# Gate and up of the second tile as a Strassen product, its z sums and all weight sums made in the first tile

## The reference, cut to what matters

```
def qlinear(x, q, scale, A, B):              # low rank part beside a quantised one
    w = (q - 7.5) * (scale * 0.005)[:, None]
    return x @ w.T + 0.02 * (x @ A @ B)
def ffn(x): return qlinear(silu(qlinear(x, gate...)) * qlinear(x, up...), down...)   # 512 -> 1376 -> 512
x = x + 0.5 * ffn(layernorm(x))
x = x + s4(layernorm(x))      # a causal convolution of each row with one kernel row of 512, and D * u
x = x + 0.5 * ffn(layernorm(x))              # the same weights
```

## Time and profile before

| | |
|---|---|
| runs | 589.48 us median of 3 (586.4, 589.48, 589.52) |
| profiled execution, its own time | 588.72 us |
| its span | 586.7 us |
| busy in the span | PE 566.7 us (97%), PEld 436.4 (74%), VectorE 403.0 (69%), ScalarE 303.2 (52%), POOL 229.5 (39%) |
| mean granted TensorE clock | 0.993 |

### The profile page before, as it was taken

One profiled execution on the slowest core, in us unless ns is written; L12 is line 12 of the kernel. 1 busy time (PEld: TensorE's weight loads), 2 busy tenths in 40 slices (PEclk: granted clock), 3 DMA queues, 4 the chain that ended last, 5 costly groups with the idle time before them and its releaser, 6 DMA issues.

```text
span 586.7 us, 12166 instructions
## 1 busy us (share of the span) xinstructions
PE 566.7 (97%) x4656; PEld 436.4 (74%) x4656; DVE 403.0 (69%) x766; ACT 303.2 (52%) x748; POOL 229.5 (39%) x248
## 2 busy tenths in 40 slices
PE   6799998999989999999999999999999999999996
PEld 6544675436678887888778887788877888788975
DVE  6577864886489867599576995479844888455544
ACT  5476412666238851478505784158831676236621
POOL 5446500030205980059701596026850367105510
PEclk9899998999999999999999999999999999999999
DMA  8983302003323074001820019000190202540001
GB/s 287 374 272 120 72 11 69 13 0 64 73 15 14 12 112 86 10 1 20 146 44 10 2 20 177 13 11 1 26 178 11 77 1 43 94 149 5 1 2 73
DMA packets 87266, 39.75 MB, mean 68 GB/s; under 512 B 75849, under 2 KB 80713, under 8 KB 87209
## 3 DMA queue, kind: packets, MB, share of 16 engines
q1 hardware_dynamic: 86393, 38.84, 29.5%
q10 hardware_dynamic: 816, 0.14, 0.1%
HBM read 16.42 MB, written 4.19 MB: 35 GB/s over the span
## 4 chain that ended last, share of the span: by engine, by line
PE 91%; DVE 4%; ACT 2%; issue 1%; DVEq 1%; DMA 1%; ACTq 0%
PE banks L1436 35%; PE banks L1359 28%; PE banks L1419 11%; PE banks L1401 5%; PE banks L1565 4%; PE banks L1324 3%; PE banks L1378 2%; PE banks L1395 1%; ACT p_stack L638 1%; DVEq L858 1%; DMA X<-in_x 1%; PE banks L1554 1%; DVE stats L857 1%; PE banks L1585 0%; DVE zs L869 0%
## 5 line engine op out<-in xcount | busy, mean ns | idle before, releaser
L1436 PE MATMUL banks<-xT,w 128*128 128x256 f16 (+1 forms) x1848 | 223.1, 273 | 1.3 <-DVE ring L996 1.3
L1436 PEld LDWEIGHTS banks<-xT,w 128*128 128x128 f16 (+1 forms) x1848 | 182.0, 100 | 22.7 <-issue 1.8
L1359 PE MATMUL banks<-dw,hT 128*128 128x256 f16 (+3 forms) x1408 | 184.8, 286 | 0.0
L1359 PEld LDWEIGHTS banks<-dw,hT 128*128 128x128 f16 (+1 forms) x1408 | 135.7, 98 | 35.0 <-issue 0.9
L955 DVE SCALAR_TENSOR_TENSOR work<-banks,work 128x512 f32<-128x512 f32 (+1 forms) x88 | 60.6, 689 | 59.3 <-PE banks L1401 25.5
L483 POOL TENSOR_TENSOR rstd<-veps,minus_half 128x1 f32<-128x1 f32 x32 | 19.9, 623 | 182.3 <-DVE veps L861 182.1
L1419 PE MATMUL banks<-xT,w 128*128 128x512 f16 (+1 forms) x336 | 80.0, 382 | 1.6 <-DVE work L955 0.7
L554 POOL TENSOR_TENSOR hT<-work,hT 128x512 f16<-128x512 f32 x60 | 70.8, 1181 | 5.0
L551 POOL TENSOR_SCALAR hT<-work 128x512 f16<-128x512 f32 x60 | 37.8, 630 | 89.1 <-DVE work L955 89.1
L1419 PEld LDWEIGHTS banks<-xT,w 128*128 128x128 f16 (+1 forms) x336 | 33.4, 101 | 42.3 <-ACT work L687 2.6
L638 ACT ACTIVATE p_stack<-banks 128x64 f16<-128x64 f32 x96 | 14.6, 226 | 88.2 <-PE banks L1324 83.5
(11 more groups left out here) (176 smaller groups left out, 704.0 us busy)
## 6 DMA issues: line engine op xcount, KB each, us to landing
out_x<-X SPq DMA_DIRECT2D x16, 256.0 KB, 2.6
X<-in_x SPq DMA_DIRECT2D x1, 2048.0 KB, 8.5
ring<-in_gate_q_t SPq DMA_DIRECT2D x2, 768.0 KB, 12.4
hT<-in_up_q_t SPq DMA_DIRECT2D x2, 768.0 KB, 13.1
work<-in_b SPq DMA_DIRECT2D x2, 688.0 KB, 8.8
X<-in_x SPq DMA_DIRECT2D x4, 256.0 KB, 5.1
X<-in_x SPq DMA_DIRECT2D x1, 1024.0 KB, 13.3
ring<-in_down_q_t SPq DMA_DIRECT2D x1, 1024.0 KB, 11.7
```

What stands on the lines that cost most here:

```text
L1359: last = mm(acc(j)[:, 1 - c, 0:width], hT[0:rows[m], m, a, j * P:(j + 1) * P], dw[0:rows[m], m, src], start=(m == 0 and a == 0), stop=(m = ...
L1436: last = mm(dst[0:r, 0:HH], w[:, blocks + k, cols], xT[:, a, 2 * op + k, :], start=(first and k == 0 and a == 0), stop=(k == 1 and a == 1) ...
```

## The change

- FAST is 1: tile 1 uses fast blocks. S4_TILE = 1 keeps the S4 steps at tile 1. The x transposes of tile 1 by subtiles go, four quarter transposes take their place.
- The z sums of tile 1 and all weight sums are made in tile 0, among its plain blocks and at its end.
- The S4 steps of VectorE move out of the blocks: s4_vectors ahead of the first pd_split of tile 0, s4_sums(0) and (1) to the end of tile 0, the rest ahead of the first pd_split of tile 1. The small product of the S4 vector B (`state_b`) moves into the blocks of tile 0.
- In fast tiles a p product makes its B11, B21 or T1 + B22 part only; VectorE copies B11 from PSUM (once for two subtiles) and adds (`p_sum`), and p_high and p_split read the sum. On ScalarE pd_copy 1 and 3 now stand before p_high.
- B's raw values go to the last half of X instead of `work`, loaded in two parts of columns; ScalarE makes the high half of the first, POOL that of the second. SP's load of that half of X waits for s_bw.
- The start: 96 and 28 warm matmuls for 60 and 12, another order of the first products, x_out(1) on VectorE, two z copies on ScalarE, block 1's products before the last p transpose and the low rank of block 0.

```diff
-    FAST = 2
+    FAST = 1
+    S4_TILE = 1
 # SP
+            sp.wait_ge(s_bw, 4)
             sp.dma_start(X[:, 2 * TS:SUBS, :], x_v[:, 2 * TS:SUBS, :]).then_inc(s_xrest[1], 16)
...
-                if n + 1 < FAST:
-                    sp.wait_ge(f.u_mm, (n + 1) * M)
-                    x_transposes(n + 1)
 # POOL
+            cast_gate(1)
             for g, wb in enumerate((gb_w, ub_w)):
-                pool.wait_ge(s_lrb[g], 16)
-                pool.tensor_scalar(wb[:, :], b_raw[:, g, :], B_SCALE, 0.0, ...
+                pool.wait_ge(s_lrb[1][g], 16)
+                pool.tensor_scalar(wb[:, b_parts[1]], b_raw[:, g, b_parts[1]], B_SCALE, 0.0, ...
-            for c in range(1, len(CHUNKS)):
+            for c in range(2, len(CHUNKS)):
                 cast_gate(c)
+            ln_rstd(1, 0, 1, 2, 3)
             for m in range(M):
                 if m == DQ:
-                    ln_rstd(1, 0, 1)
+                    z_low(1, 0, 0)
+                    z_low(1, 0, 1)
...
-            ln_rstd(1, 2, 3)
             s4_norms()
...
             s4_resolvents()
-            ln_rstd(2, 0, 1)
...
+            z_low(1, 1, 0)
+            z_low(1, 1, 1)
 # ScalarE, plain_blocks
-                    if n == 0 and m in (0, 2, 4):
+                    if n == 0 and m == 0:
+                        p_out(2)
+                        p_out(3)
+                    if n == 0 and m in (2, 4):
                         cast_up(1 + m // 2)
-                    if n + 1 == FAST and 3 <= m <= 6:
-                        z_high(n + 1, 0, m - 3)
+                    if 4 <= m <= 7:
+                        z_high(n + 1, 0, m - 4)
 # VectorE
+            def p_sum(n, i):
+                dve.wait_ge(f.p_mm, n * TS + i + 1)
+                after(dve, f.p_hi, n * TS + i)
+                own = slice(4 * R * (1 + i % 2), 4 * R * (2 + i % 2))
+                if i % 2 == 0:
+                    V.tensor_copy(p_b11, p_bank(n, i)[:, 0:4 * R]).then_inc(f.p_b11, 1)
+                    dve.wait_ge(f.p_b11, ((n - FAST) * TS + i) // 2 + 1)
+                V.tensor_tensor(p32, p_bank(n, i)[:, own], p_b11, ALU.add).then_inc(f.p_sum, 1)
...
+                    if m == 2:
+                        dve.wait_ge(s_xrest[0], 16)
+                    if m in (2, 3, 4):
+                        ln_stats(1, *((0, 1), (2,), (3,))[m - 2])
+                    if m in (3, 9):
+                        z_apply(1, m // 9)
+                    if m in (4, 10):
+                        z_differences(1, m // 10)
+                    if m == 5:
+                        z_sums(1, 0)
+                    if m in (5, 7):
+                        weight_sum(0, m // 7)
...
+                    if m == 8:
+                        weight_sum(1, 0, 1)
...
 # VectorE, tile's end
                 if n == 0:
+                    z_sums(1, 1)
                     s4_inverse()
+                    s4_b_copy()
+                    s4_vectors()
+                if s4:
+                    s4_sums(2)
+                    s4_roots(0)
+                    s4_roots(1)
+                    s4_fold()
                 pd_split(n, 0)
                 down_read(n, 0)
                 pd_split(n, 1)
                 if more:
+                    p_sum(n + 1, 0)
                     p_split(n + 1, 0)
...
                 down_add(n, 2)
+                if n == 0:
+                    weight_sum(3, 0, 1)
...
                 if more:
+                    p_sum(n + 1, 2)
                     p_split(n + 1, 2)
                 pd_split(n, 3)
...
                 down_add(n, 3)
+                if n == 0:
+                    s4_sums(0)
+                    s4_sums(1)
 # TensorE
+                elif i % 2 == 0:
+                    sums(0, half(B11, 0))
+                    last = sums(1, half(B21, 2))
                 else:
+                    last = sums(2, half(T1, 0) + half(B22, 2))
...
+                if n == 0:
+                    product(n, 0, 1)
+                    p_transpose(3)
+                    product(n, 1, 1)
                     for g in range(2):
+                        low_rank(n, g, 0)
...
-            warm(60)
+            warm(96)
             x_transpose(0, 0, 2)
-            warm(12)
+            warm(28)
             x_transpose(1, 1, 3)
             pe.wait_ge(s_aw, 1)
             p_product(0, 0)
+            p_product(0, 1)
             first_products(0)
             x_transpose(2, 2, 2)
-            p_product(0, 1)
+            first_products(1)
             x_transpose(3, 3, 3)
-            first_products(1)
             p_product(0, 2)
             p_transpose(0)
-            p_transpose(1)
             first_products(2)
             p_product(0, 3)
+            p_transpose(1)
             first_products(3)
             p_transpose(2)
-            p_transpose(3)
```

More of the change, by code:

```diff
@@ L223, in s4_macaron @@
         s_lr = sem("low_rank_a_loaded")
-        s_lrb = [sem(f"low_rank_b_{g}_loaded") for g in ("gate", "up")]
+        s_lrb = [[sem(f"low_rank_b_{g}_part{c}_loaded") for g in ("gate", "up")] for c in range(2)]
         s_lrd = sem("low_rank_down_loaded")
@@ L586, in _ @@
             s4_resolvents()
-            ln_rstd(2, 0, 1)
-            z_low(2, 0, 0)
-            ln_rstd(2, 2)
-            z_low(2, 0, 1)
-            ln_rstd(2, 3)
-            z_low(2, 1, 0)
-            z_low(2, 1, 1)
+            z_low(1, 1, 0)
+            z_low(1, 1, 1)
             for n in range(FAST, N2):
@@ L830, in _ @@
             cast_up(0)
-            x_out(1, 1, 3)
+            z_first_high(2)
             p_high(0, 0)
+            z_first_high(3)
+            p_high(0, 1)
+            low_rank_b_high(0)
+            low_rank_b_high(1)
             x_out(2, 2, 2)
-            p_high(0, 1)
             p_high(0, 2)
             p_out(0)
+            cast_up(1)
+            p_high(0, 3)
             p_out(1)
-            p_high(0, 3)
-            p_out(2)
-            p_out(3)
             act.wait_ge(s_scales, 1)
-            act.wait_ge(s_bw, 2)
             for n in range(N2):
@@ L1050, in fast_blocks @@
                 for m in range(M + 1):
+                    if n == S4_TILE and m == 0:
+                        dve.wait_ge(s_xrest[1], 16)
                     if m:
@@ L1097, in tile @@
                     conv_add(c * TS + 3)
-                if n == 0:
-                    s4_vectors()
                 if s4:
@@ L1102, in tile @@
                 if more:
+                    p_sum(n + 1, 3)
                     p_split(n + 1, 3)
@@ L1498, in tile @@
                 down_pass(n, 1, 1, LATE)
-                if n == 0:
-                    pe.wait_ge(s_kin, 128)
-                    for v in range(2):
-                        last = mm(bank[0][:, v:v + 1], vct[:, v, :], bp, start=True, stop=True)
-                    last.then_inc(s_bmm, 1)
                 down_low(n, 0)
@@ L1535, in tile, with state_b @@
                 down_low(n, 3)
+            def state_b():
+                pe.wait_ge(s_kin, 128)
+                for v in range(2):
+                    last = mm(bank[4][:, v:v + 1], vct[:, v, :], bp, start=True, stop=True)
+                last.then_inc(s_bmm, 1)
             def cauchy():
@@ L1553, in kernel_row @@
                     for c in range(2):
-                        last = mm(bank[0][0:1, :], fold[:, 4 + c, k:k + 1], tab[:, c, k, :],
+                        last = mm(bank[3][0:1, :], fold[:, 4 + c, k:k + 1], tab[:, c, k, :],
                                   start=(k == 0 and c == 0), stop=(k == 1 and c == 1))
```

171 lines of the change are left out of this document (77 added, 94 removed).

## The result

The changed kernel takes 594.73 us (median of 4 runs, 592.72 to 594.93) beside 587.94 us for the kernel before on the same chip (586.18 to 589.52): ratio 1.0117, 95% interval 1.0094 to 1.0139. It is 1.2% slower; the prediction said 582, faster, and its range ended at 588.

What follows compares the result with a forecast made beforehand. TensorE, carrying 91% of the chain of waits, was taken to bound the kernel. Terms -4.4 + 1.5 + 4.6 - 6.2 - 1.1 - 1.3 = -6.9 took 588.7 to 581.8, forecast 582 us, range 575.5 to 588.

Steps and rivals of the forecast that it cites:

- the first tile's end: First tile's end: POOL's norms delay VectorE, p_product(1,3) waits 3.3 us; +4.6 us, bounds -1.2 and 7.
- POOL's norms: First tile's end: POOL's s4_norms take 13.3 us and end at 73.0, with VectorE waiting for them.
- The slow clock behind a gap is paid before and after alike: First tile's end: both kernels pay the slow clock behind a gap, so nothing was charged for it.
- Start: Start, up to block 2: more warm matmuls and a new order bring block 2 earlier; -4.4 us, bounds -1 and -5.
- Rival B: Start: warm matmuls and new hand-overs hold it as long as before; -1 for -4.4, 585.2 us, chance 0.24.
- First tile's blocks: First tile's blocks: added z work delays ScalarE by 1.0 and 0.6 us; +1.5 us, bounds 0 and 2.5.
- Second tile's blocks: Second tile's blocks: Strassen's 38.40 us replaces plain's 44.63; -6.2 us, bounds -5 and -6.3.
- Second tile's end: Second tile's end: loses the dsum wait, gains from p, pays 0.5 us for S4 work; -1.1 us.
- Rival D: Second tile's end: S4 group starts only after both z_low; +2.1 for +0.5, 583.4 us, chance 0.10.
- Later boundaries: Five later tile boundaries: shorter p products gain 0.26 us each; -1.3 us, bounds -3.7 and +1.
- A (VectorE not late): First tile's end: POOL's norms finish before z_sums or PSUM reads go faster; -1.2 for +4.6, 576 us, chance 0.21.
- C: Seven boundaries: p sums stand on the path and cost 1.5 us at each; slower, 592.5 us, chance 0.06.

Runs made afterwards that it cites:

- e6: Changed kernel with only POOL's queue reordered: down casts start before the last two rstds, second z_low two casts later; 591.86 us, ratio 1.0068.
- e1: Changed kernel with VectorE's copy of the S4 product B made first, before z_sums and the reciprocal; 593.26 us, ratio 1.0107.
- e2: e1 with s4_vectors back at its old place, ahead of the last p split; 589.20 us, ratio 1.0037.
- e10: Changed kernel with conv_stats(0,2) behind pd_split(0,3) and weight_sum(3) behind p_split(1,3); 591.51 us, ratio 1.0080.
- e13: Changed kernel with the old p products, without sums on VectorE, at all seven boundaries; 589.26 us, ratio 1.0049.
- A: As a kernel: the changed kernel itself, against the kernel before; 594.73 us, ratio 1.0117.
- e4: Kernel before with the new start alone; second tile, S4 and p products as before; 587.98 us, ratio 1.0014.
- e12: e11 with p sums again from the fourth tile on, weight_sum(3) ahead of the reciprocal, S4 vectors behind down_add(0,2); 578.91 us, ratio 0.9852.
- e11: e9 with the old p products, without sums on VectorE, at all seven boundaries; 579.67 us, ratio 0.9876.
- e9: e8 with conv_stats(0,2) behind pd_split(0,3) and weight_sum(3) behind p_split(1,3); 583.43 us, ratio 0.9936.
- e8: Changed kernel with earlier POOL casts and memsets, b copy in block 9, vectors ahead of the reciprocal, weight sums 2 and 3 moved; 585.57 us, ratio 0.9960.

## Why the prediction was wrong

The step that failed is **the first tile's end**, +4.6 where +14.2 was measured: the length of VectorE's queue ahead of pd_split(0,0) and of p_product(1,3), with a wait on it that was not seen and a slow clock that was put at nothing. "VectorE waits there ... then reciprocal 1.74, b copy, s4_vectors 2.4 ...: 78.0. Behind them stands pd_split(0,0) ... 1.4 late." The chain was right in kind (VectorE idle for POOL, then late, and p_product(1,3) waiting for p_stack), and so were several of the signs. Its sizes were not, and one wait was missing:

- POOL's norms. The forecast has them end 7.5 us behind the start of the tile's end (73.0 less the old 65.55); they end 10.3 behind it (73.52 less 63.23), 2.8 late. POOL's queue from the last rstd to the norms' end takes 29.5 us (44.04 to 73.52) where I had 25.8 (48.6 to 74.4): the norms 14.5 for 13.3, the last four casts 4.3 where I had written 3.0 (58.1 to 61.1) although my own 0.83 each makes 3.3, z_low 4.15 for 3.72. e6, which touches POOL's queue alone, gives 2.9 us back, 1.2 of it in the blocks (the tile's end starts at 62.00 for 63.23).
- The missed wait. I asked who waits for pd_split but not who waits for the b copy. The diff adds a wait on TensorE for it, ahead of the down pass of subtile 1. I had the old trace's free TensorE up to 76.78 in its place. e1 shows that this changed where TensorE stood rather than how long (593.26, and a span of 591.9 for 593.1), since VectorE is late at the next thing that it owes as well.
- VectorE's own work was under-sized. The vectors take 6.7 us and not 2.4 (moving them, e2, gives 4.1 us of the kernel's time). The sums of p and the weight sums ahead of the last split were counted; they made a wait of 4.05 for the 3.3 forecast, on top of all that came before it, and slow clock behind it (e10 gives 2.2 us back by the ratios, e13 4.0). I had the row that warned and used it at the second tile's end, where nothing was held.
- "The slow clock behind a gap is paid before and after alike": no. Before pays it once, over some 3 us (granted clock 0.63, 0.50, 0.50 and 0.67 in the four us from 93 to 97); A pays it twice: 2.75 us on 48 down matmuls (8.87 against 6.12 in e1), 1.8 on the rest of the tile's end and 2.4 on the second tile's first block (7.56 against 5.18).

The others, in order:

- **Start**, -4.4 for -5.6: right, somewhat better, since the 96 warm matmuls took 7.42 us and ended at 9.4, not 10.2. Rival B's main reason was wrong, but e4 shows the gain can be lost a few blocks on.
- **First tile's blocks**, +1.5 for +3.2. Of the two waits at ScalarE, forecast as 1.0 and 0.6, the trace has one, 0.59 behind the cast. What was missed: down_b's two instructions took 2.35 and 2.02 us beside POOL's z_low, and held block 9's up product for 1.42 us, and state_b's matmuls (0.6) now stand here and not in the tile's end. "The weight sums moved in here lie in VectorE's free time" was true only without POOL. In e6, where z_low lies elsewhere, that wait is gone.
- **Second tile's blocks**, -6.2 for -4.3. The matmuls are as forecast; 2.4 us of slow clock stand in the first block. With the clock up (e12) the second tile takes 67.80 from start to start, 94.59 to 162.39.
- **Second tile's end**, -1.1 for +0.4. Rival D's cost did not occur: h_low was held (1.52 us for 0.68), the S4 group began at 153.60, 0.5 behind the end of POOL's z_low, ran unheld, and TensorE did not wait for it. The p sums cost here: p_split(2,2) comes late behind them, p_product(2,3) waits 1.10, and the next start waits 1.45 behind S4's row split and the last p sum. e11 has neither, and its stretch from the second to the third start is 2.0 shorter than e9's.
- **Later boundaries**, -1.3 for -1.6: right in mechanism and size (0.25 each).
- **Rivals.** A (VectorE not late) was the opposite of what happened, and at 0.21 too likely given that the queue "adds up with little idle time". C had VectorE late to the sums, which holds at two boundaries, those at which S4's work shares the queue, and not at seven. No case had TensorE waiting inside the down passes, and the upper bound of this stage, +7, had no room for the points above.

What the loss consists of is shown by runs, and on TensorE it adds up: 10.9 us more idle (7.15 + 4.05 + 1.38 for 1.63 and some 0.1) and 3.4 more busy. How much of it each edit is worth by itself is not shown, as the savings overlap (by the ratios e1 and e2 together give 4.7 us, e13 alone 4.0, e6 alone 2.9, e10 alone 2.2, each with about 1.5 us of uncertainty), since each shortens the same queue.

## What to carry to other kernels

Read a diff for every added wait, and for each name the instruction that signals it and all that stands ahead of that instruction in its queue, back to the engine that feeds it; a tiny copy behind a slow wait is as late as the wait. Then ask what the waiting engine would meet next: with this wait gone, e1 was no faster. When several edits add work to one engine between two fixed points, add up the queue there with the durations it has beside the other engines' work, not with those of a quiet stretch. And test a saving separately at boundaries where another job shares the queue: the same edit won 0.25 us at each of five and lost about 5 us over two by the medians (3.8 between e9 and e11, and the 1.25 won). In the two profiles 3.4 of it are later starts; the 1.6 of slow clock in e9's third tile may be chance.

## What the hardware showed

- VectorE and POOL hold each other, both ways, by up to 2 us an instruction. On VectorE, beside z_low's instructions of some 2 us: an fp32 TENSOR_SCALAR of 128x2 2.17 us (0.22 alone), db_w's TENSOR_SCALAR 2.35 (0.83 in e6), four halves of a weight sum 6.14 (3.3 alone), there beside the resolvents too. On POOL: a TENSOR_SCALAR of 128x256 3.48 us beside a weight sum (1.44 in e6), although it had started 1.0 us ahead of the sum (67.75, 68.79), and the sum kept its 1.64. In e8 VectorE's 128x512 reads of PSUM beside z_low (78.82 and 79.42) kept their 0.68. The Trainium skill, "GPSIMD Engine Reference", section 1 "Specifications", names VectorE's instructions with two SBUF inputs or in a 2-port mode as those that contend; the weight sums, with two SBUF inputs, fit that. Whether the two TENSOR_SCALARs ran in a 2-port mode no row here shows.
- The granted clock does not follow from the last wait alone. Behind 1.63 us it was 0.50 before; in e4, behind 1.62 us at the same place with the same matmuls ahead of it, it stayed at 1.00 (windows from 92 to 98). In e12 a wait of 1.59 us left it at 1.00:

```profile
93.00:95.00 2.00, 0.41 (x5) 1.00 0.19 40
95.00:97.00 2.00, 2.00 (x21) 1.00 0.47 132
```

  The third tile's start, with its wait of 1.54 us, was slow in two of seven profiles. So one and the same wait cost 1.6 us or nothing, and a difference of that size between two single executions can be the clock's. What decides was not tried.
